# Values of two key tiles in one run of matmuls, and the first maximum ahead of the residual's additions, in the last attention of a two-layer decoder

## What is computed

```python
qh = (q @ Wq + bq).reshape(B, LQ, 16, 16).transpose(0, 2, 1, 3)
kh = (k @ Wk + bk).reshape(B, LKV, 16, 16).transpose(0, 2, 1, 3)
vh = (v @ Wv + bv).reshape(B, LKV, 16, 16).transpose(0, 2, 1, 3)
scores = einsum('bhqd,bhkd->bhqk', qh, kh) * 16 ** -0.5
out = einsum('bhqk,bhkd->bhqd', softmax(scores), vh)
x = layernorm(x + out.transpose(0, 2, 1, 3).reshape(B, LQ, 256) @ Wo + bo)
```

## Time and profile before

| | |
|---|---|
| median of 3 runs | 1512.67 us (1511.65 to 1512.72) |
| the profiled execution's own time | 1512.28 us |
| its span, first to last instruction | 1510.5 us |
| busy over the span | PE 91%, PEld 51%, DVE 70%, ACT 51%, POOL 22% |
| mean granted TensorE clock | 0.948 of full speed |
| this attention's groups, first scores to last copy of an output | 911.31 to 1428.05 us of the span |

### The profile page before, as it was taken

How to read it: one execution, slowest core, us unless ns; L and a number is a source line. 1 busy time by engine, 2 the same in 40 slices (tenths; PEclk the granted TensorE clock), 3 DMA queues, 4 the chain that set the end, 5 groups by cost and what they waited for, 6 DMA issues and landing times. The chain is left out here.

```text
span 1510.5 us, 24918 instructions
## 1 busy us (share of the span) xinstructions
PE 1374.6 (91%) x9358; PEld 763.6 (51%) x9358; DVE 1060.9 (70%) x2349; ACT 774.5 (51%) x1066; POOL 325.4 (22%) x409
## 2 busy tenths in 40 slices
PE   6898899989999979748998888999999999999996
PEld 3565488847898966413334522333333333333285
DVE  4886566661212228667994887999999999997077
ACT  2344366621111102315764315788887888888754
POOL 4110322252000027643334550000000000000011
PEclk9999899999999989858999968999999999999999
DMA  9548533366898822774430650233322234320001
GB/s 341 186 149 244 157 131 122 125 214 214 272 301 283 295 96 60 200 204 127 135 93 21 189 185 1 67 76 98 89 66 66 66 92 97 75 66 2 1 1 56
DMA packets 153353, 198.69 MB, mean 132 GB/s; under 512 B 16235, under 2 KB 125311, under 8 KB 153106
## 3 DMA queue, kind: packets, MB, share of 16 engines
q1 hardware_dynamic: 141516, 165.34, 36.5%
q0 software_dynamic: 9200, 29.64, 6.4%
q10 hardware_dynamic: 2518, 2.13, 0.4%
HBM read 136.08 MB, written 60.70 MB: 130 GB/s over the span
## 5 line engine op out<-in xcount | busy, mean ns | idle before, releaser
L2127 DVE TENSOR_REDUCE xa_part<-psum 128x1 f32<-128x512 f32 (+1 forms) x768 | 462.5, 661 | 24.8 <-PE psum L1980 22.7
L2079 ACT ACTIVATE xa_P<-psum 128x1024 f32<-128x1024 f32 (+1 forms) x416 | 403.2, 1020 | 103.5 <-PE psum L2004 102.9
L2004 PE MATMUL psum<-sa_Q,xa_K 48*128 48x512 bf16 (+3 forms) x1664 | 266.7, 380 | 4.0 <-DMA sa_Q<-xa_mrow 2.9
L1980 PE MATMUL psum<-xa_K,sa_Q 48*128 48x512 bf16 (+1 forms) x768 | 239.0, 388 | 4.5 <-DVE xa_part L2127 1.5
L2020 PE MATMUL psum<-xa_P,xa_V 128*32 128x512 f32 (+1 forms) x1664 | 222.6, 607 | 0.4 <-ACT xa_P L2079 0.4
L1980 PEld LDWEIGHTS psum<-xa_K,sa_Q 48*128 48x128 bf16 x768 | 59.2, 94 | 232.5 <-DVE xa_part L2127 160.7
L2004 PEld LDWEIGHTS psum<-sa_Q,xa_K 48*128 48x128 bf16 (+3 forms) x1664 | 105.3, 97 | 69.0 <-ACT xa_P L2079 21.2
L2124 DVE CUSTOM_DVE_ANT_0 psum<-psum,cf_sb 128x512 f32<-128x512 f32 (+3 forms) x256 | 119.5, 522 | 25.7 <-PE psum L1980 24.7
L1328 PEld LDWEIGHTS psum<-xtT,wgu 128*128 128x128 f32 x992 | 115.5, 192 | 5.8 <-issue 4.6
L1328 PE MATMUL psum<-xtT,wgu 128*128 128x128 f32 x992 | 115.9, 275 | 1.4 <-issue 0.8
L2079 ACT ACTIVATE sa_P<-psum 128x1024 f32<-128x1024 f32 (+3 forms) x128 | 83.4, 702 | 44.0 <-PE psum L2004 43.9
(11 more groups left out here) (243 smaller groups left out, 2141.7 us busy)
## 6 DMA issues: line engine op xcount, KB each, us to landing
wgu<-in_f_gu SPq DMA_DIRECT2D x31, 1024.0 KB
xa_K<-kx SPq DMA_DIRECT2D x192, 100.1 KB, 5.1
wdn<-in_f_dn SPq DMA_DIRECT2D x31, 512.0 KB
vx<-xv_v SPq DMA_DIRECT2D x48, 256.0 KB, 3.4
xa_V<-vx POOLq DMA_DIRECT2D x16, 768.0 KB, 6.4
sa_Q<-qs SPq DMA_DIRECT2D x64, 96.0 KB, 2.3
sa_K<-ks SPq DMA_DIRECT2D x64, 96.0 KB, 2.3
sa_Q<-qx SPq DMA_DIRECT2D x64, 96.0 KB, 2.3
```

The costliest lines, as they stand in the source:

```text
L1980: last = pe.matmul(out[:, 0:width], hb.q(u)[tile:tile + HALF, to, qt * P:(qt + 1) * P], hb.k(u)[tile:tile + HALF, to, cut[e]:cut[e] + widt ...
L2004: last = pe.matmul(out(j), hb.k(u)[tile:tile + depth, to, kt * P:kt * P + r], hb.q(u)[tile:tile + depth, to, q0(kt):L], start=(half == 0), ...
L2079: act.activation(Pr[0:r, (u * KT + kt) % PR, h:h + 2, 0:w_], S_PS(p)[0:r, :, 0:w_], ACT.Exp, scale=SCALE).then_inc(s_exp, 1)
L2127: dve.tensor_reduce(part[:, g % 2, col + qt, e:e + 1], src[:, 0:cut[e + 1] - cut[e]], AX, ALU.max).then_inc(s_1free, 1)
```

## The change

In the cross-attention TensorE no longer makes the values of one key tile at each key tile. At the even tiles 2, 4, ... 12 it makes those of the two tiles before, one behind the other; at the odd tiles it makes none; at tile 0 it makes the last tile of the group before, as it did. The causal attention, which goes through the same function, keeps its order. And GpSimd runs `parts(0)`, the split of the first group's maxima, ahead of its 16 additions to the residual, where it ran behind them.

```diff
                 if not causal:
+                    parts(0)
                     for t in range(T):
                         last = pool.tensor_tensor(env.x[:, t, :], env.x[:, t, :], env.w["x_bo"], ALU.add)
                     last.then_inc(s_xb, 1)
                     pool.wait_ge(s_xb, 1)
-                    for g in range(GROUPS):
+                    for g in range(1, GROUPS):
                         if 2 <= g <= GROUPS - R + 1:
                             reload_v(g - 2, (g - 2) % R)
                         parts(g)
...
                                 scores(g, u, kt, 0, first)
                             elif turn == 1:
                                 scores(g, u, kt, 2, first)
-                            elif kt >= 1:
+                            elif causal and kt:
                                 values(g, u, kt - 1, first)
-                            elif before:
+                            elif kt and kt % 2 == 0:
+                                values(g, u, kt - 2, first)
+                                values(g, u, kt - 1, first)
+                            elif kt == 0 and before:
                                 values(g - 1, (u + R - 1) % R, KT - 1, None)
```

## The result

The changed kernel takes 1582.9 us (1581.84 to 1583.73), 1.0463 times the kernel before (95% interval 1.0446 to 1.0479): 70 us slower, where 1586 was predicted.

A forecast was written before the change was run, and what follows sets the result against it. TensorE and VectorE were both taken as within 4% of their limit, fed by a stock of three PSUM banks. 1512.28 + 78 for joined values - 4 for the earlier first maximum = 1586 us, own range 1572 to 1600.

The forecast's parts named there:

- The joined run: TensorE's values of two key tiles in one run: four passes of 0.45 us plus 0.10 exit, 1.90 us.
- The hole and the pair: VectorE gets its next unit 1.03 us late behind joined values; a pair of key tiles takes 5.67 us, 0.85 more.
- Groups 1 to 13: Middle groups of the cross-attention: 36.7 us each for 31.82, +4.9 a group, +63.5 us for 13.
- Group 0: First group, 10 units a pair with VectorE already setting the pace: +0.8 us a pair, six times, +4.8 us.
- Group 14: Second-last group, units for two thirds of it: 4 x 0.85 + 2 x 0.9, +5 us.
- Group 15: Last group, no units, ScalarE paces and waits 0.9 us more for scores, six times, somewhat less at the end: +5 us.
- The first maximum: Ahead of group 0: split moved before the additions, shift at 903.9, held by a bank; 4.2 us gained, bounds 0 and 4.7.
- What hides the additions: GpSimd's 10.9 us of additions run beside group 0, hidden: its next duty is 30 us later and VectorE isn't slowed.
- Drains win: Rival: TensorE alone sets the pace, saved switches between array shapes give some 18 us, time 1490 us; chance 6%.
- evacuation hides it: Rival: VectorE's 30.4 us a group is a floor, so TensorE's saving is lost; 1490 to 1512 us; chance 3%.
- The clock falls: Rival: TensorE, only 82% at work, gets its clock halved in pairs, some 3 us each; above 1650 us; chance 4%.
- Scores have room in this: Step in the 5.67 us pair: matmuls need 2.64 us and ScalarE's exponentials some 4, so scores don't set the pace.

The follow-up runs named there:

- e1: Changed kernel with its GpSimd part undone: joined values alone, additions back ahead of the first maximum; 1585.75 us, ratio 1.0486 to the kernel before.
- e2: Kernel before with only the first group's maximum split moved ahead of GpSimd's additions, values single; 1509.63 us, ratio 0.9976.
- e6: Kernel before with joined values and VectorE's reductions cut to 128 columns; 1566.96 us.
- e5: Kernel before, values single, with VectorE's reductions cut to 128 columns; 1498.34 us.
- e8: Kernel before with joined values, VectorE's reductions cut to 128 columns and ScalarE's exponentials to a quarter of the columns; 1509.60 us.
- e9: Kernel before with joined values, whole reductions, and ScalarE's exponentials cut to a quarter of the columns; 1580.19 us.
- e4: Kernel before with both tiles' values at the even tile but apart, each run between two units, none at odd tiles; 1590.17 us, ratio 1.0515.
- e11: Kernel before with the first maximum moved ahead and, in the last group, values of two tiles back between the scores calls; 1510.09 us, ratio 0.999.

## Why the prediction was right, point by point

- **The joined run** takes 1.86 us (1116.59 to 1118.45), 1.90 predicted: behind the first, the passes start 0.43 us apart, not 0.45.
- **The hole and the pair.** 5.58 us for 5.67. In the hole the next reduction starts 1118.85, where 1117.9 was wanted: 0.9 us late for 1.03.
- **Groups 1 to 13:** 36.45 for 36.7, +60 us for +63.5. The sum comes out this near in part by luck. The plain pairs (5.58 for 5.67) and the three tiles around tile 0 (7.99 for 8.12) are shorter than put down, together 0.6 us in a group. The shift was sized too small: 0.2 us was kept for it, and its pair is 0.56 us longer than the others. **Group 0** from its first scores to the copy of its output: 45.4 us before, 50.0 after, +4.6 for +4.8. **Group 14:** 30.0 to 34.6, +4.6 for +5. **Group 15:** +6.2 for +5, with 1.55 of the clock in it. Sum +75.4 for +78; e1 has +74.
- **The first maximum:** shift at 902.98, 1.4 us behind the maximum; from the maximum to the scores 4.2 us gained, as predicted, held by the bank and not by GpSimd. By e2, 3.6 us.
- **What hides the additions** held: e2's groups keep their 31.82 us.
- **"Drains win" and "evacuation hides it".** Both fell, and they fell further than I had put it. I wrote that the first would need units to start in time or a fourth bank. e6 has VectorE out of the way and is 69 us slower than its partner e5. The saving of entry and exit is real (0.16 us a pair in e8, 0.19 predicted) and in no run here does any of it reach the time.
- **"The clock falls"** came true once, in the last group, where I had looked for it in the pairs, and cost 1.6 us. In the 13 groups the granted clock stayed at 1.00 with TensorE marked busy for 434.87 of 473.81 us.
- **The step that was incomplete** is "Scores have room in this". I had checked that step by sums: 2.64 us of matmuls, some 4 of exponentials, both under 5.67. Their order makes a chain of 5.54. It changes the number by nothing, since the longer chain counts, but the reason given was half of the reason. For groups 14 and 15 I did name this chain, and did not carry it over to the others. By e9 and e6 either chain alone costs nearly all of the loss, so they may not be added.

Still open are the wait in e8's pair with the shift, and what makes the granted clock fall at the start of the last group.

## What to carry to other kernels

When a run of one kind of work is made longer in a queue that feeds other engines, ask for each of them how long it can live on what is in its buffers: banks times pace, against the stretch in which the feeder delivers less than is used. Count over the whole stretch, not over one run (e4). Then look for a second consumer in the same place: sums of busy time don't show a closed chain, and removing one bound shows the next only if it is really removed (e6, e9). The saving that was aimed at, 0.16 us in 4.8, could be read beforehand as entry and exit of a run; the stock that it endangers was three banks of 0.58 us.

## What the runs showed of the hardware

A switch between 64-row tiles and 32-column tiles costs, by differences of starts, 0.09 us in and 0.10 out in the earlier trace rows, and 0.16 us for both in e8. Fp32 values of 512 columns in four column tiles take 0.43 to 0.45 us a pass. The granted clock fell in the last group, which I had not expected: TensorE waited 0.80 and 0.31 us within 1.3 us, and the run behind that shows 0.58 over 4 us; in e11 it waited 0.68 and 0.80 us in the same place and its next run took 1.93 us for 1.06, with a granted clock of 0.57 from 1398 to 1402 us. The waits alone don't account for it: later in the same group TensorE waits 0.74 and 0.31 us ahead of the next joined run (1473.02 and 1473.94), and that run takes 1.92 us. From 1464 to 1468 us, ahead of the fall, TensorE was marked busy for 2.77 us. Which difference counts, no run here shows.
